# Waits for landing between groups of eight indirect DMAs in a gated cross-attention layer with a sparse expert FFN

## The reference, cut to what matters

```python
x = x + tanh(g_xattn) * attention(layernorm(x), ctx, ctx)          # 16 heads
xf = layernorm(x)
logits = xf @ Wg                                                    # 16 experts
topi = top_k(logits, 2);  gates = softmax over those two
y = sum over e of (silu(xf @ W1[e] + b1[e]) * (xf @ W11[e] + b11[e]) @ W2[e] + b2[e]) * gates[:, e]
z = silu(xf @ Ws1 + bs1) * (xf @ Ws11 + bs11) @ Ws2 + bs2           # shared expert, hidden width 1024
x = x + tanh(g_ffn) * (y + z)
```

## Time and profile before

| | |
|---|---|
| median of 3 runs | 658.24 us (657.84 to 658.49) |
| the profiled execution's own time | 662.39 us |
| its span, first to last instruction | 660.0 us |
| TensorE busy, matmuls | 563.4 us (85%) |
| TensorE weight loads | 445.7 us (68%) |
| VectorE busy | 348.3 us (53%) |
| GpSimd busy | 338.4 us (51%) |
| ScalarE busy | 213.5 us (32%) |
| mean granted TensorE clock | 0.951 |
| indirect DMAs | 64, 971 ns busy each for the scatters (L1332), 956 to 961 ns for the gathers (L1365) |

### The profile page before, as it was taken

The page is one execution under the profiler, slowest core; times in us unless marked ns, Lnnn a source line. Parts: engine busy times, 40 slices in busy tenths (PEclk is TensorE's granted clock), DMA queues, the critical chain, the costliest instruction groups (busy, mean ns, idle before and its releaser), DMA issues.

```text
span 660.0 us, 11681 instructions
## 1 busy us (share of the span) xinstructions
PE 563.4 (85%) x3146; PEld 445.7 (68%) x3147; DVE 348.3 (53%) x845; ACT 213.5 (32%) x740; POOL 338.4 (51%) x284
## 2 busy tenths in 40 slices
PE   5789898989979990498999999999999998832997
PEld 4456665656657770386888888888888886622876
DVE  5467787777655710124566655665566652101663
ACT  0687687677771100021222222222222221100110
POOL 4477888898793277130446574544547200772000
PEclk9799999999999995599999999999999999975999
DMA  6661000000205022302356776575562101331003
GB/s 231 266 244 33 18 25 25 24 16 24 81 17 223 25 103 103 120 0 77 116 184 245 273 274 226 183 253 203 205 221 82 46 25 34 106 105 43 0 1 127
DMA packets 32319, 76.05 MB, mean 115 GB/s; under 512 B 4896, under 2 KB 21408, under 8 KB 29344
## 3 DMA queue, kind: packets, MB, share of 16 engines
q1 hardware_dynamic: 12944, 51.52, 21.4%
q10 hardware_dynamic: 16272, 15.74, 7.5%
q0 software_dynamic: 3072, 8.39, 4.0%
HBM read 54.93 MB, written 18.61 MB: 111 GB/s over the span
## 4 chain that ended last, share of the span: by engine, by line
PE 69%; another core or an unknown queue 10%; DVE 8%; issue 5%; POOL 3%; ACT 2%; DMA 1%; DVEq 0%; SPq 0%; ACTq 0%; POOLq 0%
PE mid L646 12%; PE big L627 7%; PE big L629 7%; PE big L628 7%; PE work L402 5%; PE last L567 4%; PE work L567 3%; PE big L551 3%; PE big L549 3%; PE big L550 3%; PE mid L637 3%; PE big L431 3%; PE work L417 2%; PE work L611 2%
## 5 line engine op out<-in xcount | busy, mean ns | idle before, releaser
L709 ACT ACTIVATE arena<-big,nmax 128x128 f32<-128x128 f32 x256 | 90.3, 398 | 4.8 <-DVE nmax L880 4.8
L646 PE MATMUL mid<-dring,arena 128*128 x376 | 88.9, 379 | 0.0
L774 ACT ACTIVATE last<-arena 128x512 f32<-128x512 f32 x47 | 28.3, 602 | 185.5 <-DVE arena L1142 185.5
L627 PE MATMUL big<-u_hi,xsT_hi 128*128 x188 | 82.9, 441 | 1.7 <-issue 1.7
L1142 DVE TENSOR_TENSOR arena<-big,bring 128x512 f32<-128x512 f32 x47 | 32.5, 692 | 89.2 <-PE big L629 89.2
L1035 DVE SCALAR_TENSOR_TENSOR arena<-big,bias,arena 128x512 f32<-128x512 f32 x32 | 23.8, 749 | 99.7 <-ACT arena L759 91.8
L567 PE MATMUL last<-dring,arena 128*128 128x256 f32 x128 | 34.2, 415 | 48.6 <-DVE x_all L1046 48.6
L759 ACT ACTIVATE arena<-big,bias 128x512 f32<-128x512 f32 x32 | 21.9, 687 | 163.6 <-PE big L551 82.5
L629 PE MATMUL big<-u_hi,xsT_lo 128*128 x188 | 74.3, 395 | 0.0
L1267 POOL TENSOR_TENSOR u_lo<-arena,u_hi 128x2048 fp32r<-128x2048 f32 x16 | 73.3, 4583 | 1.3
L1251 POOL TENSOR_TENSOR arena<-arena,rinv 128x1024 f32<-128x1024 f32 x32 | 60.7, 1898 | 25.8 <-DVE rinv L888 25.2
(11 more groups left out here) (133 smaller groups left out, 1118.2 us busy)
## 6 DMA issues: line engine op xcount, KB each, us to landing
arena<-up_w_dram SPq DMA_DIRECT2D x16, 1024.0 KB, 7.6
bring<-expert_bias_dram SPq DMA_DIRECT2D x16, 640.0 KB, 5.3
dring<-down_w_dram SPq DMA_DIRECT2D x18, 512.0 KB, 3.4
sorted_y<-arena ACTq DMA_DIRECT2D x47, 128.0 KB, 1.8
arena<-sorted_x ACTq DMA_DIRECT2D x43, 128.0 KB
sorted_x<-dring SPq DMA_DIRECT2D x3, 1536.0 KB, 8.5
dring<-up_w_dram SPq DMA_DIRECT2D x2, 1024.0 KB, 4.9
xf_all<-xfs SPq DMA_DIRECT2D x16, 128.0 KB, 2.0
```

The lines of the kernel that those rows point to most:

```text
L627: mm(big[:, p, w, :], x_hi, u_hi[:, slot, o:o + HID], start=(k == 0), stop=False)
L646: i = mm(mid[:, 1, 0:D], gT[:, p, c, :], dring[:, slot, c * D:(c + 1) * D], start=(c == 0), stop=(c == HC - 1))
L709: i = nc.scalar.activation(probs[:, u % 2, h, :], big[:, u % 2, h // 4, (h % 4) * CTX:(h % 4 + 1) * CTX], ACT.Exp, bias=nmax[:, u % 2, h:h ...
```

## The change

Behind each fourth tile of the scatter loop and of the gather loop, so behind each eight indirect DMAs, GpSimd waits until everything issued so far in that loop (scatter) or in that group (gather) has landed.

```diff
...
                 for k in range(TOPK):
                     g.indirect_dma_start(out=sorted_x, out_offset=bass.IndirectOffsetOnAxis(ap=pos[:, k, t:t + 1], axis=0),
                                          in_=xf_all[:, t, :], in_offset=None).then_inc(scattered, 16)
+                if t % GROUP == GROUP - 1:
+                    pool.wait_ge(scattered, 16 * TOPK * (t + 1))
...
                     g.indirect_dma_start(out=yg[:, t % GATHERS, k, :], out_offset=None, in_=sorted_y,
                                          in_offset=bass.IndirectOffsetOnAxis(ap=pos[:, k, t:t + 1], axis=0)) \
                         .then_inc(gathered[t // GROUP], 16)
+                if t % GROUP == GROUP - 1:
+                    pool.wait_ge(gathered[t // GROUP], 16 * TOPK * GROUP)
```

## The result

| | kernel before | changed kernel |
|---|---|---|
| median of 4 runs each, same chip | 658.37 us (657.84 to 661.80) | **612.58 us** (611.66 to 613.29) |
| ratio, 95% interval | | **0.9299** (0.9280 to 0.9319) |
| profiled execution | 662.39 us, span 660.0 | 612.34 us, span 610.0 |
| mean granted TensorE clock | 0.951 | 0.983 |

What follows compares the result with a forecast made beforehand. TensorE was taken to be held up by late done signals during GpSimd's indirect DMA bursts. −23.5 − 29.8 + 2.4 + 8.1 = −42.8 us gave 619.6 profiled, 615 us as median; own range 603 to 628, stated range 603 to 669.

Steps and rivals of the forecast that it cites:

- The cause of the two holes: TensorE nearly idle at 247 to 273 and 573 to 606 us, its done signals arriving late while GpSimd issues indirect DMAs.
- The pause, 1.43 us: Price of each GpSimd landing wait: 1.17 us more until the next issue plus 0.26; 4.3 us for three.
- the 0.26: Extra length of the first scatter after a wait, 1.22 us against 0.96, counted into each pause's price.
- bounds of 2.7 to 8.6: Range in us for three pauses, from 0.9 us a pause to 2.9 us at twice the price.
- Scatter gain, 23.5 less 2.4: First row transposes at 274.5 for 298.06 us, 23.5 us won, less 2.4 us for signals still late.
- The 5.7 us of waiting: TensorE's wait for rows behind the scatters, set against 8.1 us of remaining signal lateness, leaving 2.4.
- Gather gain, 29.8 less 8.1: `shared_ups(6)` starts at 582.8 for 612.64 us, 29.8 us won, less 8.1 us for signals still late in three groups.
- In each of the six later groups one signal late by 2.7 us: Lateness left after the pauses, three groups per burst: 8.1 us in the scatters, 8.1 in the gathers.
- The sum: Scatter and gather gains with remaining lateness: −42.8 us, profiled execution from 662.39 to 619.6 us.
- Rival A: Half relief: a pause empties only part, signals late again mid-group, half of 53.3 us won; 631 us, chance 0.22.
- Rival B: No relief, slower: signals come only after 4.8 us without an issue, pauses too short; 667 us, chance 0.35.
- B's 8.6: Rival B's added time in us: the scatter hole ends 4.3 us later and so does the gather one.

Runs made afterwards that it cites:

- e2: Changed kernel with only the gather waits, scatters as in the kernel before: 604.06 us, ratio 0.9999 to the kernel before (603.68 us on that chip).
- c1: The changed kernel word for word, on a chip where the kernel before takes 604.74 us: 611.13 us, ratio 1.0121.
- e3b: Changed kernel with a landing wait behind each sixteen indirect DMAs, not eight: 642.34 us, ratio 0.9776, with 656.75 us before on that chip.
- e1: Changed kernel with only the scatter waits, gathers as in the kernel before: 610.22 us, ratio 1.0115 to the kernel before (603.68 us on that chip).
- e5: Changed kernel with a GpSimd multiply of some 1.7 us in place of each inner landing wait: 611.62 us, ratio 0.9295, with 658.73 us before.
- e8: Changed kernel with all four tiles of the last shared group ahead of the first row transposes: 604.52 us, ratio 1.0002, with 604.74 us before.
- e8b: Changed kernel with all four last shared tiles ahead of the row transposes, on a chip with 659.15 us before: 608.20 us, ratio 0.9227.
- e10: Changed kernel with GpSimd multiplies for the landing waits and all four last shared tiles ahead of the row transposes: 605.97 us, ratio 0.9192.
- e9: Kernel before, without waits or pauses, with all four last shared tiles ahead of the row transposes: 659.86 us, ratio 1.0020, with 658.73 us before.
- e4: Changed kernel with a landing wait behind each four indirect DMAs, not eight: 618.63 us, ratio 1.0243, with 603.68 us before.

## Why the prediction was right, point by point

- **The cause of the two holes: right.** Late signals of TensorE while GpSimd issues indirect DMAs, not a missing engine or transfer. Where the signals are in time (e2), the same scatters leave no hole at all.
- **The pause, 1.43 us: right to the hundredth in the scatters, too small in sum.** Two of three gaps are 1.73 us, that is 1.43 more than 0.30, by the row of SyncE's start plus 0.26. (The prediction took the 0.26 for a longer issue behind the wait; that issue takes 0.96 us, and the 0.26 is spent in the gap.) The other, the second, is 3.77 us, and in the gathers the gaps are 2.96, 2.04 and 2.07, so that the pauses of each burst cost 6.2 to 6.3 us for the forecast 4.3, inside the bounds of 2.7 to 8.6. The Trainium skill's 2.0 us plus bytes over 436 GB/s ("DMA: Bandwidth & Descriptors", "Anatomy of one DMA — SWDGE (gpsimd) path"), an estimated 2.3 us for such a DMA, is 0.4 below the 2.69 us (0.96 + 1.73) from the start of the 8th issue to the start of the 9th.
- **Scatter gain, 23.5 less 2.4: right in size, for another reason.** It is 21.9 us, 0.6 of it because the whole burst starts earlier (225.64 for 226.28). L611 starts at 276.12 in place of the forecast 274.5, and the rows make that delay: the pauses are 2.0 us longer than forecast and SyncE's first load stands at 273.94 for 272.6. The lateness of signals (once 1.2 us on a silu, and once 1.0 on an output tile's signal, where VectorE's L1046 at 249.06 has 2.28 us before it) is covered: TensorE waits 8.67 us for the rows anyway. (The 5.7 us of waiting that the prediction set against the lateness are 6.0 by its own 274.5 and 268.5.)
- **Gather gain, 29.8 less 8.1: right in its first term, wrong in its second.** It is 27.8 us. "In each of the six later groups one signal late by 2.7 us" was too much: in the three of the gathers two are late, by 1.4 and 0.6 us. TensorE then has 1.66 us of idle before its third tile (577.98), and 0.52 us at the same place in c1, where no silu is late there, so they cost it some 1.1 us. What is missing to the 29.8 us is 2.0 us where 8.1 was put down. This is the term that was mis-sized most.
- **The sum: −42.8 forecast, −50.0 in the profiled executions.** 615 us came near to 612.58 us with some luck. The profiled time was forecast at 619.6 and is 612.3; then 4.15 us were taken off because the profile of before lay above its median, and the profile after does not. The two errors, 7.3 us one way and 4.4 the other, leave 2.9.
- **Rival A (half relief, 631 us)** did not come about, but it is what e3b shows: once signals are late, a single pause relieves little. Eight in a row is short enough, sixteen is not.
- **Rival B (no relief, slower) was wrong here; on the other kind of chip the kernel is slower, for less than B's price.** "Signals come only after 4.8 us without an issue" falls with the silus from 252.41 to 261.77 of the changed kernel, in time or 1.2 us late with no gap above 3.77 us before them. (The 4.8 us that the prediction reads in both bursts are 5.0 in the gathers, from 599.27 to 604.31.) Where there is no hold-up to relieve, the pauses cost 6.4 us (c1) for B's 8.6: all of it in the scatters, where B put 4.3, and nothing in the gathers. The Trainium skill's advice to issue early and wait late ("DMA: Bandwidth & Descriptors", "Rules for kernel authors") is borne out by c1 and e1, and reversed by e5 and the result: on those chips, issuing all 32 of a burst without a stop costs 46 to 47 us.
- **What was missed altogether:** that the hold-up is not a property of the kernel alone. The prediction took 658 us as what the chip does. On two of the four chips that the experiments ran on, the kernel before takes 604 us, and there the changed kernel loses 1.2%.

## What to carry to other kernels

If TensorE stands idle in a stretch in which GpSimd issues many indirect DMAs in a row and the chain of waits names an unknown queue, compare the start of the first waiter with the last matmul it waits for; if it is late, break the issuing up with a pause of some 1.7 us behind each eight, for which GpSimd may as well be given other work, and don't count on one pause after the lateness has begun. Measure the kernel before beside it on more than one chip, since the same change gained 7% on one and lost 1.2% on another. And put independent work of the waiting engine under the pauses: with the waits kept, that took the loss away on one kind of chip (e8) and gave 608.20 us on the other (e8b).

## What the runs showed of the hardware that was not expected

- **The same program takes 604 us on some chips and 657 to 659 us on others**, each time with a spread of 1% or less. No profile of the kernel before was taken on a chip of the first kind, but e2 has its scatters, and waits in the gathers that cost it nothing: against the profile of before, its stretch from the first scatter to L611 is 27.8 us shorter (44.02 for 71.78) and that from the first gather to the end 28.9 us (71.99 for 100.84), 56.6 of the 59.2 us between the spans. Whether the difference is a property of the chip or of a time was not settled: one chip was seen twice (658.73 and 656.75 us), the others once. What in such a chip delays TensorE's signals is open too; the runs show its onset and its relief, not its place.
- **The onset looks like a queue that fills.** At 1.27 us per issue the first signal is 1.2 us late at 12.9 us; at 1.38 us it is 0.3 us late at 17.4 us; with a pause behind each eight lateness stays under 2 us; with one behind sixteen it returns. The signals behave as if something filled up a little with each issue. This was argued from four profiles; no run measured such a queue.
- **Not tried:** waiting one group behind instead of for the last, e10 or e9 on a chip without the hold-up, pauses shorter than 1.7 us, and as many indirect DMAs with fewer bytes, which would tell the issuing from the data moved.
- **The second scatter pause is the long one** in every kernel that waits for landing behind eight: 3.77 us in the changed kernel, 3.67 in e1, 3.21 in c1, 3.84 in e8, 3.56 in e8b, with 1.72 or 1.73 for the others. In the changed kernel the only other transfer between 246 and 251 us is a packet on an instruction queue: the page's part on DMA queues for that window (packets, MB, share of 16 engines' time) has two rows:

```profile
q0 software_dynamic: 96, 0.26, 15.1%
q8 instruction: 1, 0.02, 2.2%
```

All five have such a packet between 247.2 and 250.2 us, before their 16th scatter has landed. In two kernels whose wait at this place is 1.73 us none is in the way: in e4 it ends at 249.62, before the 16th scatter's data moves (from 250.4), and in e3b it comes at 263.8. That the fetch of code delays a share of the 16th scatter is argued from this coincidence; no run moved the fetch.
